# Projecting layer 0's values for two heads at once, with tokens on the partitions

## The reference

```python
q = jnp.einsum('bpd,hde->bphe', resid_pre, W_Q) + b_Q
k = jnp.einsum('bpd,hde->bphe', resid_pre, W_K) + b_K
v = jnp.einsum('bpd,hde->bphe', resid_pre, W_V) + b_V
q = _apply_rotary(q, cos, sin)
k = _apply_rotary(k, cos, sin)
scores = jnp.einsum('bqhd,bkhd->bhqk', q, k) / ATTN_SCALE
scores = jnp.where(causal[None, None], scores, 0)
max_v = jnp.max(jnp.abs(scores), axis=-1, keepdims=True)
sgn = jnp.sign(scores)
attn_w = sgn * jnp.exp(sgn * scores - max_v)
attn = attn_w / (jnp.sum(jnp.abs(attn_w), axis=-1, keepdims=True) + 1e-06)
z = jnp.einsum('bkhd,bhqk->bqhd', v, attn)
out = jnp.einsum('bqhd,hdm->bqm', z, W_O) + b_O
```

## Time and profile before

| what | us |
|---|---|
| median of 3 runs | 904.88 |
| the runs | 900.77, 904.88, 909.34 |
| the profiled execution | 900.11 |
| its span, first to last instruction | 898.1 |
| layer 0's attention in it | about 13 to 415 |

### The profile page before, as it was taken

One profiled execution on the slowest core, in us unless ns is written; L12 is line 12 of the kernel. 1 busy time (PEld: TensorE's weight loads), 2 busy tenths in 40 slices (PEclk: granted clock), 3 DMA queues, 4 the chain that ended last, 5 costly groups with the idle time before them and its releaser, 6 DMA issues.

```text
span 898.1 us, 14700 instructions
## 1 busy us (share of the span) xinstructions
PE 837.0 (93%) x4420; PEld 629.4 (70%) x4420; DVE 631.5 (70%) x1322; ACT 552.0 (61%) x1161; POOL 474.5 (53%) x398
## 2 busy tenths in 40 slices
PE   3799999999999999887898999989999988999997
PEld 2477777887777777666787888654444346888886
DVE  4777888887888888878467865867777643576554
ACT  2688888888888888762543533335556564454442
POOL 2745566665666555443666775613310524556774
PEclk9899999999999999999999999988999999999999
DMA  4212222223423322110674547511441122344442
GB/s 133 94 65 89 93 90 90 92 94 95 148 95 95 93 93 93 57 62 20 197 250 138 188 147 263 164 39 65 136 134 63 55 73 86 115 146 130 151 150 70
DMA packets 57851, 99.90 MB, mean 111 GB/s; under 512 B 8320, under 2 KB 19072, under 8 KB 57792
## 3 DMA queue, kind: packets, MB, share of 16 engines
q1 hardware_dynamic: 57792, 99.17, 34.3%
HBM read 72.67 MB, written 9.57 MB: 92 GB/s over the span
## 4 chain that ended last, share of the span: by engine, by line
PE 73%; DVE 11%; issue 7%; POOL 4%; ACT 3%; DMA 2%; SPq 0%; DVEq 0%; ACTq 0%; POOLq 0%
PE ps L879 9%; PE ps L856 9%; PE ps L865 9%; PE ps L316 8%; PE ps L375 6%; PE ps L327 6%; PE ps L364 4%; PE ps L338 4%; PE ps L354 4%; PE ps L1542 3%; PE ps L1429 2%; DVE nm L1738 2%; PE ps L1516 2%; PE ps L1450 2%; PE ps L382 1%
## 5 line engine op out<-in xcount | busy, mean ns | idle before, releaser
L1005 POOL TENSOR_TENSOR ew_lo<-ew_raw,ew_hi 128x768 fp32r<-128x768 f32 x68 | 127.6, 1878 | 61.8 <-ACT ew_hi L970 41.8
L952 ACT ACTIVATE hid_hi<-guw 128x512 fp32r<-128x512 f32 x68 | 43.0, 632 | 158.6 <-POOL guw L1021 107.2
L1021 POOL TENSOR_TENSOR guw<-gu,cwb 128x512 f32<-128x512 f32 x64 | 84.8, 1325 | 100.5 <-issue 74.4
L1060 DVE TENSOR_TENSOR hid_lo<-guw,hid_hi 128x512 fp32r<-128x512 f32 x68 | 78.3, 1153 | 73.9 <-ACT hid_hi L952 73.8
L1738 DVE TENSOR_REDUCE nm<-ps 128x1 f32<-128x512 f32 x128 | 81.4, 684 | 27.1 <-PE ps L1450 26.8
L1633 ACT ACTIVATE e<-ps 128x512 f32<-128x512 f32 x128 | 68.9, 599 | 40.6 <-PE ps L1542 40.2
L464 DVE TENSOR_TENSOR q_rot<-ps,q_sin 128x512 f32<-128x512 f32 x64 | 44.1, 691 | 61.1 <-POOL q_sin L505 33.3
L521 POOL TENSOR_TENSOR wv_lo<-wv_raw,wv_hi 128x256 fp32r<-128x256 f32 x32 | 35.4, 1106 | 93.2 <-ACT wv_hi L452 93.2
L488 DVE SCALAR_TENSOR_TENSOR w<-ex,rden,sgn 128x512 f32<-128x512 f32 (+3 forms) x128 | 82.0, 700 | 2.9
L505 POOL TENSOR_TENSOR q_sin<-q_sw,sin 128x512 f32<-128x512 f32 x64 | 81.4, 1292 | 2.5 <-DMA q_sw<-q_in 2.5
L879 PE MATMUL ps<-ew_hi,hid_hi 128*128 128x256 f32 x272 | 78.3, 288 | 4.3 <-DVE hid_lo L1060 3.6
(11 more groups left out here) (181 smaller groups left out, 2378.3 us busy)
## 6 DMA issues: line engine op xcount, KB each, us to landing
ew_raw<-in_ew SPq DMA_DIRECT2D x68, 384.0 KB, 3.2
q_sw<-q_in SPq DMA_DIRECT2D x128, 128.0 KB, 2.0
cwb<-cw_dram SPq DMA_DIRECT2D x64, 256.0 KB, 3.5
wqk_raw<-in_wqk SPq DMA_DIRECT2D x32, 256.0 KB, 2.7
wv_raw<-in_wv SPq DMA_DIRECT2D x32, 128.0 KB, 2.2
wo_raw<-in_wo SPq DMA_DIRECT2D x32, 128.0 KB, 2.1
qs<-stk_q SPq DMA_DIRECT2D x16, 256.0 KB, 3.6
ks<-stk_k SPq DMA_DIRECT2D x16, 256.0 KB, 4.2
```

The source lines that it names most:

```text
L1005: pool.tensor_tensor(ff[f].ew[1][:, i % EW_SLOTS, :], ew_raw[:, i % RAW_SLOTS, :], fp(ff[f].ew[0][:, i % EW_SLOTS, :]), ALU.subtract).then ...
L1021: pool.tensor_tensor(ff[f].guw[:, i % 2, :], ff[f].gu[:, i % 2, :], ff[f].cwb[:, r % CWB_SLOTS, :], ALU.mult).then_inc(sem("guw"), 1)
L1060: dve.tensor_tensor(ff[f].hid[1][:, i % 2, :], ff[f].guw[:, i % 2, :], fp(ff[f].hid[0][:, i % 2, :]), ALU.subtract).then_inc(sem("hid_lo"), 1)
```

## The change

- V is computed for a pair of heads (even n and n+1). Stationary are 128 tokens of xT, and the weights of both heads move, 256 columns. Each step does two of the four token tiles of the pair: 2 x 6 matmuls of 256 columns into bank 2. The result has tokens on partitions, as PV needs it.
- vT, its eviction, VT and the copy to v0 are gone. DVE moves the half (128 x 512) from bank 2 to v0 and adds the bias in the same instruction. It stands behind w and ahead of z_lo in DVE's order, and waits for V of this step (`v_ps`) and for an earlier PV.
- S waits for `v0` of the step before (`halves_by(i - 1)`).
- The bias must lie along the columns, the same on all partitions: bv_rows, made once in steps -2 and -1 by 16 transposes of broadcast columns on PE and two ACT copies of 1024 columns.
- The split of the value weights runs four heads ahead instead of two, in two slots of two heads. ACT's wv_hi and POOL's wv_lo keep their place in the order of a step; SP issues the load behind that of wqk instead of ahead of it.
- The hardware loops have a body of four steps instead of two. Before the first logits PE also waits for a sign of the last head. bv_rows lies where the experts' hid lies later.

```diff
@@ a0_pe
                 n = i + 1
                 wait(pe, "q_rot", 2 * n + 2)
-                wait(pe, "v_ev", n)
-                wait(pe, "v0", n)
+                wait(pe, "v0", halves_by(i - 1))
+                if known(n) and n == 0:
+                    pe.wait_ge(sem("bv_rows"), 1)
...
-            if valid(i + 1, N0):
-                n = i + 1
+            if valid(pair_head(i), N0):
+                n = pair_head(i)
                 b = n // H0 if known(n) else batch[0]
-                wait(pe, "wv_lo", n + 1)
-                wait(pe, "sgn", of_tile(n + 1, 3))
-                for j in range(3 * DC):
-                    c, (pw, px) = j // 3, PARTS[j % 3]
-                    last = pe.matmul(ps[:, 2, :], wv[pw][:, c, :], (xT_hi, xT_lo)[px][:, c, b * S:(b + 1) * S],
-                                     start=j == 0, stop=j == 3 * DC - 1)
+                wait(pe, "wv_lo", n + 2)
+                if valid(i + 1, N0):
+                    wait(pe, "sgn", of_tile(i + 2, 3))
+                for t2 in range(2):
+                    t = 2 * odd() + t2
+                    for j in range(3 * DC):
+                        c, (pw, px) = j // 3, PARTS[j % 3]
+                        last = pe.matmul(ps[:, 2, t2 * D:(t2 + 1) * D], (xT_hi, xT_lo)[px][:, c, b * S + t * P:b * S + (t + 1) * P],
+                                         wv[pw][:, slot_of(2 - odd()), c, :, :].rearrange("p k d -> p (k d)"),
+                                         start=j == 0, stop=j == 3 * DC - 1)
                 last.then_inc(sem("v_ps"), 1)
...
-                wait(pe, "v0", n + 1)
+                wait(pe, "v0", n + 2 - odd())
                 wait(pe, "wT_ev", 3 * n + 3)
                 for j in range(QT):
-                    last = pe.matmul(ps[:, 7, j * P:S], v0[:, j * P:(j + 1) * P], wT[:, j, j * P:S],
+                    last = pe.matmul(ps[:, 7, j * P:S], v0[:, slot_of(0), j, odd() * DH0:(odd() + 1) * DH0], wT[:, j, j * P:S],
                                      start=j == 0, stop=j == QT - 1, skip_group_check=True)
                 last.then_inc(sem("pv"), 1)
-            if valid(i + 1, N0):
-                n = i + 1
-                wait(pe, "v_ev", n + 1)
-                for t in range(QT):
-                    last = pe.transpose(ps[:, 4, t * P:(t + 1) * P], vT[:, t * P:(t + 1) * P], ident[:, :])
-                last.then_inc(sem("vt_ps"), 1)
@@ a0_act
-                wait(act, "v_ps", n + 1)
-                wait(act, "vt_ps", n)
-                act.activation(vT[:, :], ps[:, 2, :], ACT.Identity,
-                               bias=bqkv0[:, 2, bass.ds(n, 1)]).then_inc(sem("v_ev"), 1)
...
-                wait(act, "vt_ps", n + 1)
-                wait(act, "pv", n)
-                act.activation(v0[:, :], ps[:, 4, :], ACT.Copy).then_inc(sem("v0"), 1)
-            if valid(i + 2, N0):
-                n = i + 2
+            if valid(i + 4, N0):
+                n = i + 4
                 wait(act, "wv_ld", 16 * (n + 1))
-                wait(act, "v_ps", n)
-                act.activation(wv[0][:, :, :], wv_raw[:, :, :], ACT.Copy).then_inc(sem("wv_hi"), 1)
+                wait(act, "v_ps", i + 2 - odd())
+                act.activation(wv[0][:, slot_of(4), :, odd(), :], wv_raw[:, :, :], ACT.Copy).then_inc(sem("wv_hi"), 1)
@@ a0_dve, behind the four products that make w, ahead of z_lo
+            if valid(pair_head(i), N0):
+                n = pair_head(i)
+                col = (n % H0 if known(n) else n - batch[0] * H0) * DH0
+                wait(dve, "v_ps", halves_by(i))
+                wait(dve, "pv", i - odd())
+                if known(i) and i in (-2, 2):
+                    dve.wait_ge(sem("bv_rows"), 1 if i < 0 else 2)
+                dve.tensor_tensor(v0[:, slot_of(2 - odd()), 2 * odd():2 * odd() + 2, :],
+                                  ps[:, 2, :].rearrange("p (t d) -> p t d", t=2),
+                                  bv_rows[:, bass.ds(col, 2 * DH0)].unsqueeze(1).broadcast_to([P, 2, 2 * DH0]),
+                                  ALU.add).then_inc(sem("v0"), 1)
@@ a0_sp
-            if valid(i + 2, N0):
-                n = i + 2
-                src = a["wv0"][head(n)]
-                wait(sp, "wv_lo", n)
-                sp.dma_start(wv_raw[:, :, :], src).then_inc(sem("wv_ld"), 16)
             if valid(i + 4, N0):
                 n = i + 4
                 src = a["wqk0"][head(n)]
                 wait(sp, "wqk_lo", n)
                 sp.dma_start(wqk_raw[:, :, :, :], src).then_inc(sem("wqk_ld"), 16)
+                src = a["wv0"][head(n)]
+                wait(sp, "wv_lo", n)
+                sp.dma_start(wv_raw[:, :, :], src).then_inc(sem("wv_ld"), 16)
@@ a0_steps
-                    with eng.Fori(i // 2, last // 2) as r:
-                        for k in range(2):
-                            odd[0] = 1 - k
-                            step(eng, 2 * r + 1 + k)
+                    with eng.Fori((i - 3) // 4, (last - 2) // 4) as r:
+                        for k in range(4):
+                            quarter[0] = (3 + k) % 4
+                            step(eng, 4 * r + 3 + k)
+        def pair_head(i):
+            return i + 2 - odd()
+
+        def halves_by(i):
+            return i + 3
+        def bias_rows(pe, k):
+            for h in range(8 * k, 8 * k + 8):
+                last = pe.transpose(ps[:, BV_BANK[k] + h % 8 // 4, h % 4 * P:(h % 4 + 1) * P],
+                                    bqkv0[:, 2, h:h + 1].broadcast_to([P, P]), ident[:, :])
+            last.then_inc(sem("bv_ps"), 1)
```

More of the change, by code:

```diff
@@ L106, in build_program @@
         wv_raw = sb("wv_raw", [P, DC, DH0])
-        wv = [sb(f"wv_{p}", [P, DC, DH0], F32R) for p in ("hi", "lo")]
+        wv = [sb(f"wv_{p}", [P, 2, DC, 2, DH0], F32R) for p in ("hi", "lo")]
         wo_raw = sb("wo_raw", [P, D])
@@ L113, in build_program @@
         q_rot = sb("q_rot", [P, 2, 2, S])
-        vT = sb("vT", [P, S])
-        v0 = sb("v0", [P, S])
+        v0 = sb("v0", [P, 2, QT, 2 * DH0])
         sabs = sb("sabs", [P, QT, S])
@@ L123, in build_program @@
         rden = sb("rden", [P, QT])
+        ones_r = sb("ones_r", [P, S], F32R)
         wT = sb("wT", [P, QT, S])
         z0 = [sb(f"z0_{p}", [P, S], F32R) for p in ("hi", "lo")]
-        ones_r = sb("ones_r", [P, S], F32R)
         l0_end = cursor[0]
@@ L135, in ffn_large @@
             r.guw = sb(f"guw{f}", [P, 2, S])
+            r.hid_at = cursor[0]
             r.hid = [sb(f"hid{f}_{p}", [P, 2, S], F32R) for p in ("hi", "lo")]
@@ L191, in build_program @@
         late_end = cursor[0]
+        cursor[0] = ff[0].hid_at
+        bv_rows = sb("bv_rows", [P, H0 * DH0])
+        assert cursor[0] <= late_end and late >= l0_end
+        cursor[0] = late_end
         ffn_small(small)
@@ L333, in a0_pe @@
                 wait(pe, "wo_lo", n + 1)
+                if first and n == 0:
+                    pe.wait_ge(sem("bv_rows"), 2)
                 if first and n > 0:
@@ L517, in a0_pool @@
                 pool.tensor_tensor(wo[1][:, :], wo_raw[:, :], fp(wo[0][:, :]), ALU.subtract).then_inc(sem("wo_lo"), 1)
-            if valid(i + 2, N0):
-                n = i + 2
+            if valid(i + 4, N0):
+                n = i + 4
                 wait(pool, "wv_hi", n + 1)
-                pool.tensor_tensor(wv[1][:, :, :], wv_raw[:, :, :], fp(wv[0][:, :, :]),
+                pool.tensor_tensor(wv[1][:, slot_of(4), :, odd(), :], wv_raw[:, :, :], fp(wv[0][:, slot_of(4), :, odd(), :]),
                                    ALU.subtract).then_inc(sem("wv_lo"), 1)
@@ L548, in a0_sp, with odd, slot_of @@
                 sp.dma_start(wqk_raw[:, :, :, :], src).then_inc(sem("wqk_ld"), 16)
+                src = a["wv0"][head(n)]
+                wait(sp, "wv_lo", n)
+                sp.dma_start(wv_raw[:, :, :], src).then_inc(sem("wv_ld"), 16)
         batch = [0]
-        odd = [0]
+        quarter = [0]
         LOOPS0 = {3: (H0 - 6, 0), H0 + 3: (N0 - 6, 1)}
         def par(ahead):
-            return (odd[0] + ahead) % 2
+            return (quarter[0] + ahead) % 2
+        def odd():
+            return quarter[0] % 2
+        def slot_of(ahead):
+            return (quarter[0] + ahead) // 2 % 2
+        def pair_head(i):
+            return i + 2 - odd()
+        def halves_by(i):
+            return i + 3
         def a0_steps(eng, step, at=None, i=-4):
@@ L561, in a0_steps @@
                     last, batch[0] = LOOPS0[i]
-                    with eng.Fori(i // 2, last // 2) as r:
-                        for k in range(2):
-                            odd[0] = 1 - k
-                            step(eng, 2 * r + 1 + k)
+                    with eng.Fori((i - 3) // 4, (last - 2) // 4) as r:
+                        for k in range(4):
+                            quarter[0] = (3 + k) % 4
+                            step(eng, 4 * r + 3 + k)
                     i = last + 1
                 else:
-                    odd[0] = i % 2
+                    quarter[0] = i % 4
```

(13 more changed lines are left out.)

9 lines of the change are left out of this document (removed).

## The result

The changed kernel takes 932.02 us (median of 4 runs, 929.88 to 934.16), the kernel before beside it on the same chip 904.14 (900.77 to 909.34): ratio 1.030, 95% interval 1.0245 to 1.0362. It is 27.9 us slower. The profiled execution took 929.88 us, its span is 928.2, clock 0.98; so beside the profile of before (900.11) the difference is 29.8. In what follows the medians count every run, and the ratios leave out two that lay over 1.5% above the fastest of their kernel (910.96 us, one of the four with the addition ahead of w, and 2020.42 us, one of the twelve with the new order, for which nothing on record gives a cause).

A forecast was written before the change was run, and what follows sets the result against it. PE bounds the kernel before; then S waits for the addition behind w, step 12.04 us. Steady 17.0, start 4.5 and end 1.3 make 22.8 on 900.11: 922.9; on the median 927.7, said 927. Range 908 to 944, forecast's own 918 to 937.

The forecast's parts named there:

- the second loop: From one S to the next through ScalarE's eight, mask, w and addition: 11.6 us, less than 12.04, so not deciding.
- The loop over two periods: Steady heads: Q to S of the next step 15.92 us, S to next Q 8.16; together two periods, 12.04 each.
- the half prices: Steady step: both legs together span two periods, so time added to one leg costs half of it per period.
- ScalarE's part: Two evictions go, 0.689 and about 0.58 us; freeing ScalarE moves DVE by little, so nothing was taken.
- Rival B: No change in the steady step: ScalarE's 1.27 us come off the chain, step 11.41, only start and end paid: 911; 9%.
- TensorE's part: PE's step: four transposes gone, 0.44 us; V in 256-column matmuls +0.03; net -0.41, 11.00 us if PE stays the bound.
- Steady: Scores of head 2 to head 29: 0.63 us more in each of 27 intervals, +17.0.
- Start: S of head 1 waits for w of head 0 and runs at low clock; S of head 2 at 58.0, not 53.5: +4.5.
- End: Heads 30 and 31: each addition again in DVE's chain, +0.6 for each of two, PE's later S giving back: +1.3.
- A: Faster: S isn't late, PE stays the bound and loses 12.7 us, giving 892; 6%.
- C: Slower still: the 1.04 us gap before each S puts PE's clock back to 0.50, +32, 959; 4%.
- D: Bare weight loads: six added loads of 0.188 us on PE's leg, half of it per period, +15, 942; 2%.

The follow-up runs named there:

- new order: Kernel after, with the addition between cosine products and rotation's sums and TensorE's order Q, S, first transposes, V, other transposes, O, PV: 898.07 us, ratio 0.993.
- ordering alone: Kernel before, with one wait more: S of the next head waits until w of this head is written; no addition. 944.63 us, ratio 1.041.
- and wo_hi late: Kernel after with the addition made twice, and ScalarE's copy of the output weights (wo_hi) moved behind the exponentials: 966.39 us, ratio 1.070.
- both splits behind w: Kernel after with addition twice and wo_hi behind the exponentials, plus GpSimd's wo_lo waiting until w is written, wv_lo queued behind it: 940.31 us, ratio 1.036.
- eviction put back: Kernel after, with an unread ScalarE copy of the values' bank ahead of the exponentials, from step 3 to step 26 only: 947.15 us, ratio 1.048.

## Why the prediction was right, and where its steps were wrong

The time was right: 927 forecast, 932 measured, inside the forecast's own range. The signs listed for it came too: TensorE busy 0.91, steps of 12.1, the addition at 0.68, V at 1.44, w at 2.42. **The cause** was right too: w and S no longer overlap, since S waits for an addition behind w. The run with the addition ahead of w takes the whole loss away, and the one with the ordering alone brings it without the change.

**The loop was the wrong one.** What failed is the sentence on the second loop, from one S to the next: "11.6, less than 12.04 [...] It doesn't decide." I led it through ScalarE's signs, the mask and the maxima. But ahead of the exponentials ScalarE also evicts the transposed weights, which wait for T, which stands behind S and O on TensorE, and then copies wo_hi. In the rows above that is 171.21 to 177.10, 5.89 us. Mine needed 0.96 + 2.73 + 0.86 = 4.55 to the maxima and 0.88 from there to the exponentials, which began at 163.24 in the kernel before:

```profile
163.24 1.91 ACT L436 ACTIVATE ex<-sabs,nmax 128x512 f32<-128x512 f32 x4
```

That makes 5.43, and the 0.46 that is missing turns the forecast's 11.63 into 12.09. Loop by loop, in us, each from starts in one step of that kernel's trace; the last column is how long after the maxima the exponentials start:

| kernel | S to exponentials | to w | to next S | sum | step | behind the maxima |
|---|---|---|---|---|---|---|
| after | 5.89 | 3.09 | 3.12 | 12.10 | 12.11 | 0.82 |
| addition twice | 5.90 | 3.10 | 3.85 | 12.85 | 12.84 | 1.19 |
| and wo_hi late | 5.58 | 3.47 | 3.85 | 12.90 | 12.90 to 12.94 | 0.86 |
| and both splits behind w | 5.66 | 3.15 | 3.37 | 12.18 | 12.17 | 0.71 |
| eviction put back | 6.88 | 3.04 | 2.91 | 12.83 | 12.83 | 2.16 |
| ordering alone | 7.08 | 3.03 | 2.48 | 12.59 | 12.56 to 12.69 | 2.15 |

A sum of distances around a loop gives the step in any case; what shows the loop is that each edit changed one leg by its own full size (addition +0.73, eviction +0.99, wo_hi -0.32), and that the rest stood but for VectorE's instructions that met a split of GpSimd's more or less than before (-0.21, +0.37). The last column says the same step by step. Where nothing on ScalarE holds the exponentials, they start 0.71 behind the maxima: that is the median in the runs with the addition ahead of w, with wv_lo or both splits behind w, with the transposes put back and with the new order. In the kernel after it is 0.81 to 1.04 in most steps, so there they wait for ScalarE's queue.

The loop over two periods that I had, 12.04, is there as well, a little below: taking back what was added, the runs put it at 12.30 - 0.22 = 12.08 (transposes back) and 12.17 - 0.36 + 0.24 = 12.05 (both splits behind w). In the kernel after the maxima start at 176.28, behind q_rot, and the first one takes 0.68 (mean of that shape), so it is there at 176.96, 0.14 ahead of the exponentials. It decides where the other is shortened (wv_lo behind w, both splits behind w) or it alone is lengthened (the transposes put back). So 12.04 was near 12.11 because two loops nearly tie, which is luck, and the half prices failed wherever the loop from S to S was lengthened: ordering alone, addition twice, eviction put back.

**ScalarE's part** I took at nothing: "freeing ScalarE moves DVE by little". That holds only while S comes early. With S late, the eviction stands in front of the exponentials, and its return costs 0.72 us a step, 15 us in all. Rival B had the right mechanism, but its gain only keeps a worse 12.83 at 12.11; it doesn't reach back to 11.41.

**TensorE's part**: V's form 0.05 (forecast 0.03), and 11.05 us as the step where TensorE is the bound (11.00). Weight loads: their rows lie beside the matmuls, and the run with V in 256 columns says so in time. The section of the Trainium skill that the prediction cites ("TensorE: Matmul & The Clock Gate", "The mechanism") names a second case beside another row group, a load into the background weight buffer; whether that is the case here, no run shows. **The addition** took 0.68 (0.69), and S followed its end by 0.10 (0.05).

**The sizes.** Steady: +19.3 for +17.0, mainly 0.70 a step for 0.63. Start: +6.3 for +4.5; w of head 0 began 2.1 later (39.04 against 36.93) where I had 1.1, and took 6.79 for 6.32, and S of head 1 began at 46.53 for 45.1 and took 4.57 for 4.1, at a granted clock of 0.52:

```profile
46.53 4.57 PE L331 MATMUL ps<-q_rot 128*128 128x512 f32 x8 [9.58 <-issue]
...
59.85 2.40 PE L331 MATMUL ps<-q_rot 128*128 128x512 f32 x8 [0.87 <-issue]
```

End: +1.5 for +1.3, but by another cause: the clock alone is 1.6, so the additions there cost nothing on balance, and that the size fits is luck. **The other rivals**: A needed the addition 2.1 us sooner. Moved ahead of w it is off the way, and the step is 11.05. C: no clock loss in gaps of 0.8 (granted 1.00), only at the start and at the end. D is out.

## What to carry to other kernels

When a new wait couples two engines, write down every loop that it closes, with all that stands in front of each instruction on its own in-order queue, also what has slack today: an eviction of 0.7 us in front of the exponentials was nearly free in the kernel before and cost 15 us once S came late. To tell which of two nearly equal loops binds, double a term and see whether the step grows by all of it or by half; and try an instruction that someone waits for ahead of the long group it stands behind.

## What the runs showed of the hardware

Some VectorE instructions that read SBUF alone ran longer beside a split of GpSimd's, and the split too. The 384-column product of w took 1.04 us in the mean where wv_lo lies beside it and 0.61 without; dene took 0.57 for 0.17; wv_lo itself took 0.80 beside w and 0.73 elsewhere. The addition and z_lo, whose first operand is in PSUM, took 0.68 to 0.69 beside a split or alone. I had used the 1.096 of the earlier trace rows as an upper bound for the addition, and had not seen that moving a split off w was worth 13 us, nearly half of the 27.9 lost. The Trainium skill ("SBUF — State Buffer", "Who interferes with whom") says that an instruction of VectorE with two SBUF inputs contends with one of GpSimd that reads SBUF, and one with at most one SBUF input doesn't, outside the two-port modes. The rows of w, of the addition and of z_lo agree. dene reads one operand of 4 elements and was held all the same. The section counts `tensor_scalar`, which dene is, among the instructions that can enter such a mode; whether this one did, no run here shows. What the rows show is that dene ended (178.10) with wo_lo (178.07).

The granted clock did not follow the length of the idle time alone. S took 2.40 us behind 2.62 of idle time in the kernel before, 3.82 behind 2.69 in the kernel after, and in the run with the addition ahead of w it is twice 4.08:

```profile
373.89 4.08 PE L331 MATMUL ps<-q_rot 128*128 128x512 f32 x8 [2.40 <-issue]
387.50 4.08 PE L331 MATMUL ps<-q_rot 128*128 128x512 f32 x8 [2.55 <-issue]
```

The granted clock of these S was 1.00, 0.60, and twice 0.58, where 0.50 is the lower of the two levels. With the values' transposes put back the last S took 2.40 behind 2.53, at 1.00. So 2.40 us of idle time went before a slow S and 2.53 and 2.62 before fast ones. What else sets it, these runs don't show.
